# Attention with softmax maxima added by matrix products: the products on halves of the array, their transposes at later places, and a tail of zeros written by scatters

## The reference

```python
def _L0_xattn_ref(q, k, v, wq_w, wq_b, wk_w, wk_b, wv_w, wv_b, wo_w, wo_b):
    # H = 16 heads of DH = 8 channels
    wq = (q @ wq_w.T + wq_b).reshape(b, t, H, DH)
    wk = (k @ wk_w.T + wk_b).reshape(b, t, H, DH)
    wv = (v @ wv_w.T + wv_b).reshape(b, t, H, DH)
    scores = jnp.einsum('bthd,bshd->bhts', wq, wk) / jnp.sqrt(jnp.float32(DH))
    probs = jax.nn.softmax(scores, axis=-1)
    attn = jnp.einsum('bhts,bshd->bthd', probs, wv)
    return attn.reshape(b, t, d) @ wo_w.T + wo_b

def _L0_ffn_ref(x, Wg, W1, W2, W3):
    # E = 8 experts, TOP_K = 2
    logits = xf @ Wg
    top_w, top_i = jax.lax.top_k(logits, TOP_K)
    top_w = jax.nn.softmax(top_w, axis=-1)
    combine = jnp.einsum('nk,nke->ne', top_w, jax.nn.one_hot(top_i, E))
    h = jnp.einsum('nc,ech->enh', xf, W1)
    g = jnp.einsum('nc,ech->enh', xf, W2)
    y = jnp.einsum('enh,ehc->enc', jax.nn.silu(h) * g, W3)
    out = jnp.einsum('enc,ne->nc', y, combine)

x = x + jnp.tanh(g_xattn[0]) * _L0_xattn_ref(_layernorm(x), ctx, ctx, ...)
x = x + jnp.tanh(g_ffn[0]) * _L0_ffn_ref(_layernorm(x), ...)
```

## Time and profile before

| | |
|---|---|
| median of 3 runs | 519.75 us |
| lowest and highest | 516.56 and 519.78 us |
| the profiled execution | 516.52 us |
| its span | 514.4 us |
| PE, matmul busy | 465.3 us, 90% of the span |
| DVE busy | 388.0 us, 75% |
| ACT busy | 301.9 us, 59% |
| POOL busy | 222.6 us, 43% |
| mean granted clock | 0.993 |

### The profile page before, as it was taken

The page is one execution under the profiler, slowest core; times in us unless marked ns, Lnnn a source line. Parts: engine busy times, 40 slices in busy tenths (PEclk is TensorE's granted clock), DMA queues, the critical chain, the costliest instruction groups (busy, mean ns, idle before and its releaser), DMA issues. The chain is left out here.

```text
span 514.4 us, 14505 instructions
## 1 busy us (share of the span) xinstructions
PE 465.3 (90%) x4462; PEld 380.5 (74%) x4462; DVE 388.0 (75%) x1684; ACT 301.9 (59%) x755; POOL 222.6 (43%) x311
## 2 busy tenths in 40 slices
PE   2479999999999999899799999998998989899997
PEld 1257877777777787677687788767897877777996
DVE  4567788988889888767468658676799886677974
ACT  2377777777777775545365565466544547453553
POOL 2322155556565444545000177562668762224420
PEclk9999999999999999999899999999999999999999
DMA  8701001100001110135465344320000221000011
GB/s 245 299 11 53 13 32 41 38 31 36 36 31 37 34 52 24 43 114 164 135 180 168 97 134 124 91 78 24 22 27 16 57 57 48 11 2 1 1 42 42
DMA packets 45022, 34.60 MB, mean 67 GB/s; under 512 B 5922, under 2 KB 41122, under 8 KB 44708
## 3 DMA queue, kind: packets, MB, share of 16 engines
q1 hardware_dynamic: 30036, 20.55, 13.4%
q0 software_dynamic: 4128, 8.40, 5.3%
q10 hardware_dynamic: 10800, 4.92, 3.3%
HBM read 21.86 MB, written 11.99 MB: 66 GB/s over the span
## 5 line engine op out<-in xcount | busy, mean ns | idle before, releaser
L482 POOL DMA_INDIRECT sent<-xr,rowu x60 | 59.1, 986 | 67.6 <-DVE rowu L1041 53.6
L498 POOL DMA_INDIRECT yg<-done,gidx x64 | 64.3, 1004 | 31.5 <-issue 16.6
L1260 DVE TENSOR_TENSOR act<-sil,bank 128x256 f32<-128x256 f32 x71 | 29.8, 420 | 28.7 <-ACT sil L697 25.8
L931 DVE TENSOR_REDUCE mx<-bank 128x8 f32<-128x512 f32 x64 | 41.1, 683 | 11.0 <-PE bank L1694 11.0
L697 ACT ACTIVATE sil<-bank 128x256 f32<-128x256 f32 x71 | 27.3, 384 | 36.5 <-PE bank L1868 36.5
L464 POOL TENSOR_TENSOR ve<-mv,half 128x4 f32<-128x4 f32 (+1 forms) x40 | 8.9, 221 | 86.5 <-DVE mv L855 83.8
L1884 PE MATMUL bank<-f0w_s,aT 128*128 x284 | 45.1, 282 | 0.8 <-DVE yb L1266 0.8
L636 ACT ACTIVATE Pr<-bank 128x512 f32<-128x512 f32 x64 | 34.7, 597 | 13.5 <-PE bank L1708 13.5
L1884 PEld LDWEIGHTS bank<-f0w_s,aT 128*128 128x128 f32 x284 | 38.2, 195 | 1.7 <-issue 1.2
L1694 PE MATMUL bank<-QK 64*64 64x256 f32 x512 | 36.4, 401 | 2.9 <-ACT QK L626 2.9
L800 ACT ACTIVATE hg<-bank 128x512 f32<-128x512 f32 x32 | 19.1, 598 | 30.0 <-PE bank L2042 26.5
(11 more groups left out here) (253 smaller groups left out, 1309.6 us busy)
## 6 DMA issues: line engine op xcount, KB each, us to landing
xb<-sent SPq DMA_DIRECT2D x71, 64.0 KB
done<-yb ACTq DMA_DIRECT2D x71, 64.0 KB
cT<-ctx_t_dram SPq DMA_DIRECT2D x16, 128.0 KB
f0w_s<-f_w_dram SPq DMA_DIRECT2D x1, 2048.0 KB, 11.0
Pr<-ctx_t_dram SPq DMA_DIRECT2D x8, 256.0 KB
QK<-ctx_tok_dram SPq DMA_DIRECT2D x8, 256.0 KB
out_dram<-xs SPq DMA_DIRECT2D x8, 256.0 KB, 2.3
xs<-x_dram SPq DMA_DIRECT2D x2, 512.0 KB, 5.7
```

What stands on the lines that cost most here:

```text
L482: nc.gpsimd.indirect_dma_start(sent, bass.IndirectOffsetOnAxis(ap=rowu[:, s, 2 * k + c:2 * k + c + 1], axis=0), rows[:, c, :], None).then_ ...
L498: nc.gpsimd.indirect_dma_start(yg[:, s, j, :], None, done[0:NG1 * P, :] if u < UG else done, bass.IndirectOffsetOnAxis(ap=gidx[:, s, j:j + ...
L931: nc.vector.tensor_reduce(mx[:, g, :], bank[SC_BANK[g]][:].rearrange("p (m k) -> p m k", k=L), AX, ALU.max).then_inc(S("a_max"), 1)
```

## The change

What it does, by the pieces of the diff:

- `mxs` becomes 128 x 128 for each j, in a part of QK that nothing else uses in the attention. Its columns 0 to 7 and 8 to 15 hold the rounded maxima and their rests of g = 2j, columns 64 to 79 those of g = 2j + 1, and POOL writes zeros into the others once. The transpose (`a_mt`) takes all 128 columns, and ACT copies 128 partitions. So the maxima of g = 2j lie on partitions 0 to 63 and those of g = 2j + 1 on 64 to 127, and each product of `a_less` takes 64 rows as weights and 64 of the one `own_m` left.
- ACT no longer fills `mxT` with zeros and writes one version of `own_m`.
- `a_mt(u + 1, 0)` stands behind `r_lg(u - 2)` instead of ahead of it. `a_mt(u + 1, 1)` stood at the end of iteration u; now it stands in iteration u + 1 between the transposes of g = 0 and g = 1, and ACT's copy between the copies of g = 0 and g = 1.
- SP's `zero_after` is gone. `tail` has the row for each partition and expert, and POOL scatters 8 x 128 rows of zeros behind the last unit's sends, which no longer wait for blocks 13 to 16.

```diff
@@ constants
-    c[np.arange(32), C_MB + np.arange(32) % 16] = 1
+    c[p, C_MB + p % 8] = p % L < 16
@@ tiles
-        mxs = sb("mxs", [P, 2, 2, 16], F32R)
+        mxs = QK[:, U4 // 4, 0:2 * P].rearrange("p (j x) -> p j x", j=2)
...
-        tail = sb("tail", [1, E], U32)
+        tail = sb("tail", [P, E], U32)
@@ SP
-                sp.wait_ge(S("a_s"), 2 * UA)
+                sp.wait_ge(S("a_mt"), 2 * UA)
...
-            def zero_after(e):
-
-                if e == 0:
-                    sp.wait_ge(S("tail"), 1)
-                r = sp.value_load(tail[0:1, e:e + 1], min_val=e * REGION, max_val=e * REGION + TOKENS)
-                sp.dma_start(sent[bass.ds(r, P), :], zero[:]).then_inc(S("tails"), 16)
...
-                if 16 <= t < 16 + E // 2:
-                    zero_after(2 * (t - 16))
-                    zero_after(2 * (t - 16) + 1)
@@ POOL
+            nc.gpsimd.memset(mxs[:], 0.0).then_inc(fill, 1)
...
-            send(UA - 1, 1, (13, 14, 15, 16))
+            def zero_after(first, last):
+
+                for e in range(first, last):
+                    nc.gpsimd.indirect_dma_start(sent, bass.IndirectOffsetOnAxis(ap=tail[:, e:e + 1], axis=0), zero[:], None).then_inc(S("tails"), 16)
+
+            pool.wait_ge(zeroed, 16 * E)
+            send(UA - 1, 1)
+            wait_alone(pool, S("tail"), 1)
+            zero_after(0, E)
@@ ACT
-            for r in range(2):
-                nc.scalar.activation(own_m[:, r, :].rearrange("p (m k) -> p m k", k=L),
-                                     cst[:, C_MB + 8 * r:C_MB + 8 * r + 8].unsqueeze(2).to_broadcast([P, 8, L]), ACT.Copy)
-                nc.scalar.activation(mxT[:, r, :], ident, ACT.Copy, scale=0.0)
+            nc.scalar.activation(own_m[:, 0, :].rearrange("p (m k) -> p m k", k=L),
+                                 cst[:, C_MB:C_MB + 8].unsqueeze(2).to_broadcast([P, 8, L]), ACT.Copy)
...
-                nc.scalar.activation(mxT[0:32, j, :], bank[MT_BANK[j]][0:32, 0:P], ACT.Copy, scale=-1.0).then_inc(S("a_mts"), 1)
+                nc.scalar.activation(mxT[:, j, :], bank[MT_BANK[j]][:, 0:P], ACT.Copy, scale=-1.0).then_inc(S("a_mts"), 1)
...
                     a_pts(u, 0)
+                    a_mts(u, 1)
                     a_pts(u, 1)
...
-                if has(u + 1):
-                    a_mts(u + 1, 1)
@@ DVE
-                nc.vector.tensor_copy(mxs[:, j, 0, :], some).then_inc(S("a_ms"), 1)
+                nc.vector.tensor_copy(high.bitcast(F32R), some).then_inc(S("a_ms"), 1)
...
-                nc.vector.tensor_tensor(mxs[:, j, 1, :], some, mxs[:, j, 0, :], ALU.subtract).then_inc(S("a_ms"), 1)
+                nc.vector.tensor_tensor(low.bitcast(F32R), some, high, ALU.subtract).then_inc(S("a_ms"), 1)
...
-                    nc.vector.tensor_copy(tail[:], run[0:1, :]).then_inc(S("tail"), 1)
+                    nc.vector.tensor_scalar(tail[:], run[:], cst[:, C_P:C_P + 1], None, ALU.add).then_inc(S("tail"), 1)
@@ PE
-                nc.tensor.transpose(bank[MT_BANK[j]][0:32, 0:P], mxs[:, j].rearrange("p h m -> p (h m)").bitcast(F32), ident).then_inc(S("a_mt"), 1)
+                nc.tensor.transpose(bank[MT_BANK[j]][:, 0:P], mxs[:, j, :], ident).then_inc(S("a_mt"), 1)
...
-                    mm(bank[SC_BANK[2 * j + r]][:], mxT[:, j, :], own_m[:, r, :], start=False, stop=True,
+                    mm(bank[SC_BANK[2 * j + r]][:], mxT[L * r:L * (r + 1), j, :], own_m[L * r:L * (r + 1), 0, :], start=False, stop=True,
...
                     a_pt(u, s, 0)
+                    a_mt(u, 1)
                     a_pt(u, s, 1)
...
+                if has(u - 2):
+                    r_lg(u - 2)
                 if has(u + 1):
                     a_mt(u + 1, 0)
-                if has(u - 2):
-                    r_lg(u - 2)
...
-                if has(u + 1):
-                    a_mt(u + 1, 1)
```

More of the change, by code:

```diff
@@ L69 @@
 C_MB = C_QM + 2
-C_N = C_MB + 16
+C_N = C_MB + 8
 R_BO, R_BQV, R_BG = 0, 128, 256
@@ L407, in _ @@
                 if u == 1:
-                    sp.wait_ge(fill, 10)
+                    sp.wait_ge(fill, 11)
                     for e in range(E):
@@ L456, in _ @@
             nc.gpsimd.memset(w1c[:], 0.0).then_inc(fill, 1)
+            nc.gpsimd.memset(mxs[:], 0.0).then_inc(fill, 1)
             pool.dma_start(f0g_s[:], f0_wg).then_inc(ld_f0g, 16)
-            pool.wait_ge(fill, 10)
+            pool.wait_ge(fill, 11)
             def rstd(k, u, n):
@@ L648, in _ @@
             a.wait_ge(prep, 3)
-            a.wait_ge(fill, 10)
+            a.wait_ge(fill, 11)
             def r_xts(v):
@@ L897, in _ @@
             v.wait_ge(ld_attn, 64)
-            v.wait_ge(fill, 10)
+            v.wait_ge(fill, 11)
             nc.vector.tensor_copy(bvb[:], colv[:, BV:BV + 1].to_broadcast([P, P]))
@@ L933, in a_split @@
             def a_split(u, j):
-                some = mx[:, 2 * j:2 * j + 2, :].rearrange("p g m -> p (g m)")
+                some = mx[:, 2 * j:2 * j + 2, :]
+                high, low = (mxs[:, j, :].rearrange("p (r x) -> p r x", r=2)[:, :, 8 * k:8 * k + 8] for k in range(2))
                 v.wait_ge(S("a_max"), u * 4 + (2 * j + 2))
-                nc.vector.tensor_copy(mxs[:, j, 0, :], some).then_inc(S("a_ms"), 1)
+                nc.vector.tensor_copy(high.bitcast(F32R), some).then_inc(S("a_ms"), 1)
                 v.wait_ge(S("a_ms"), u * 4 + (2 * j + 1))
-                nc.vector.tensor_tensor(mxs[:, j, 1, :], some, mxs[:, j, 0, :], ALU.subtract).then_inc(S("a_ms"), 1)
+                nc.vector.tensor_tensor(low.bitcast(F32R), some, high, ALU.subtract).then_inc(S("a_ms"), 1)
             def a_rec(u):
```

## The result

| | before | changed |
|---|---|---|
| median | 518.86 us of 6 runs (516.56 to 519.97) | 507.29 us of 6 runs (504.81 to 507.94) |
| ratio | | 0.977, interval 0.974 to 0.980 |
| profiled execution, span | 516.52, 514.4 us | 504.81, 502.9 us |
| start of the expert stage's block 0 | 210.33 us | 204.71 us |
| block 18 to block 21 | 9.39 us | 5.26 us |

The change makes the kernel 11.6 us faster by the medians. The starts of PE's first transpose of a block split the 11.5 us that the profiled execution's span lost: 5.6 in the attention, 4.1 between blocks 18 and 21, and 1.8 that no part of the change accounts for, 0.75 between blocks 0 and 18 (35.85 us before, 35.10 now) and 1.0 behind block 21 (258.83 and 257.83). In the first of these stretches the granted clock of before stood at 0.50 for 3.4 us (from 217.4); the changed kernel's profiled execution has no such fall.

What follows compares the result with a forecast made beforehand. PE's queue, busy 90% of the span, was taken as the bound. Terms 3.8 + 3.4 + 1.1 + 4.4 = 12.7 us gave 503.8 from the profiled execution or 507.0 from the median; forecast 505.5 us, range 502 to 510.

Steps and rivals of the forecast that it cites:

- The halves, 3.8 us: Attention: 512-column product pairs on array halves save 0.22 and 0.02 us, 16 units x 0.24 = 3.8 us on PE's path.
- The later places, 3.4 + 1.1: Attention: moving the maxima's transposes later cuts PE's waits, 3.4 us over four loop pairs and 1.1 us outside the loop.
- none at the turn: At the loop's turn, PE would have no wait left before the transposed maxima; elsewhere at most 0.4 us.
- DVE just keeps up: Attention loop: of DVE's slack, some 1.4 us a pair, the gains use 1.3, so DVE would not hold PE back.
- The rival on DVE's pace: Attention loop: DVE sets the pace, its eight units gain nothing, 5.3 us are lost, time 511; chance 0.12.
- The zeros, 4.4: Expert stage, blocks 18 to 21: zeros moved from SP to POOL save 4.9 us, less 0.5 stall at block 25: 4.4.
- The clock's share included: Expert stage: the 4.9 us gain at blocks 18 to 21 includes time from a halved clock lasting some 2 us.
- Halves in sequence: Rival, attention: the two half-array products run one after the other, costing 7 us, time 512.5; chance 0.12.
- the slow case: Rival, attention: half arrays handle the reduced float type at the float rate, 17 us lost, time 527; chance 0.06.
- Cheaper changes of form: Rival, attention: changes of tiling form cost less and the turn gives all it has, 3.7 us more, 502; chance 0.05.
- Late zeros: Rival, expert stage: zeros come too late, a 3 us stall at block 25 and a clock fall cancel 4.4; 510; chance 0.05.
- The starting point: Whole kernel: gains taken from the profiled 516.5 us give 503.8, from the 519.75 median 507.0; 505.5 chosen between.

Runs made afterwards that it cites:

- last sends behind blocks: The changed kernel with the last unit's two sends waiting for blocks 13 to 16 again, as before the change; 507.69 us, ratio 0.977.
- POOL's step moved: The changed kernel with POOL's 128 x 512 subtraction for the gate's weights (w12_low) moved from behind the sends to between two small steps, units 1 to 8; 504.9 us.
- fastest kernel: The changed kernel with POOL's w12_low subtraction moved beside the maxima and four DVE bookkeeping steps moved behind the first split of the maxima; 502.41 us, ratio 0.966.

## Why the prediction was right, and where it was not

The time (507.3 for 505.5) came out within the range. The terms did so less evenly, and in part it was luck: the attention gave 5.6 us (5.9 from unit 0 to unit 15) for 8.3, and 1.8 us of the profiled gain of 11.5 came where no term had counted anything.

*The halves, 3.8 us: the step that failed.* "16 units x 0.24", "on PE's path", is right in its size, 0.28 measured in the late units, 0.25 of it in the first pair and 0.03 in the second, and wrong in the path: it holds only where PE has no wait behind it. Alone the halves gave 0.1% by the ratio, 0.4 us, and that can't be told from nothing. On top of the places they bring block 0 from 206.22 to 204.71, 1.5 us, and unit 0 to unit 15 from 166.50 to 164.79, 1.7 us: 0.4 of this in the loop's eight units and 1.3 in the others.

*The later places, 3.4 + 1.1.* From unit 0's product with the values to unit 15's it is 170.67 us before and 166.23 with the places alone: 4.4 us, for 4.5. Inside, the sum was off both ways. The loop's units gave 4.0: a pair fell by 1.04 us (23.98 to 22.94) and not by 0.84. The edges gave 0.5 for 1.1. At the start the covered wait fell by 0.58 us (1.84 to 1.26), but the next one grew by 0.40 (0.97 to 1.37). Behind the loop, units 11 to 15 take 41.05 us before and with the places: the wait of 0.73 only made room for one for DVE's table, which stands ahead of the ranks (0.58 with the places alone; the line is the changed kernel's),

```profile
166.34 0.18 PE L1762 MATMUL bank<-chosen,upb 128*128 128x8 bf16 x1 [0.53 <-DVE table L1142]
```

and the first transpose's later place cost 0.36 in the iteration of unit 14 (193.49 above, 0.37 there). No queries and keys are left to be made in it, and the logits, which stood between the transpose and the pair of products, now stand ahead of both, so the pair waits for ACT's copy. The prediction had no term for this. Of the waits that were to be left, the one of 0.4 is 0.22 (at 114.55); "none at the turn" missed by 0.19.

*"DVE just keeps up".* It is where the prediction should have stopped. DVE's slack was counted once for both gains and taken to be free for either. It belonged to the ring, and the places used it up; there was none for the halves. The rival on DVE's pace named this, but with a price of 5.3 us ("the loop's eight units gain nothing"). From unit 3 to unit 11 they gained 4.2 of these 5.3 (95.22 to 91.03). Loop pairs of 22.7 were said, 22.90 came.

*The zeros, 4.4.* 4.1 us between blocks 18 and 21 (9.39 to 5.26), and as much in the kernel with the zeros alone. Two terms were off and nearly cancelled. Three blocks take 5.26 and not 4.5, so less was there to win. And no stall came at block 25. The margin hardly changed: from the last zeros' issue to PE's block 25 it is 6.8 us (244.2 to 251.0), where the prediction had 6.1. What differs is the load, taken to need 3.4 us, which was there within 2.04 of its issue in the kernel with the last sends behind blocks. "The clock's share included" was not needed, and the fall lasted 3.4 us and not some 2: the kernels with the halves or the places alone take 9.2 us there at a granted clock of 1.00. The gap is SP's lost lead; the low clock of the earlier trace rows took the place of a part of the waiting.

*The rivals.* Halves in sequence and the slow case fell: both products of the reduced type stream at once, at the rate of the whole array. (The slow case's own sum gives 526, not 527.) Cheaper changes of form fell with the 0.03 us of the second pair. Late zeros need 3 us more.

*The starting point.* Between 503.8 and 507.0 the prediction took the middle. The changed kernel's profiled execution is its fastest (504.81, clock 1.00), and the others, at 0.99 to 0.997, lie 0.9 to 3.1 us above; the median stands at 507.3. The 12.7 of the sum against the median of all runs of before, 518.86, would have given 506.2.

## What to carry to other kernels

When two engines wait for each other in turn, their waits are one ring and not two stores of slack: ask for every saving whether it lies on the stretch from one engine's wait to what it hands over, for else it only lengthens the next wait. A gain that shows in the written-out units and not in the loop is the sign of it; it comes back in full once the ring is shorter than the engine's own work, as the halves did here (0.27 us a unit in the loop). To get there, take out of the chain between the two engines what no one nearby needs, and look for operations that take much longer in the loop than outside, as the subtraction of 0.16 us did that took up to 1.32.

## What was not expected of the hardware

- A VectorE subtraction of 128 x 2 with both inputs in SBUF took 0.88 to 1.32 us beside a GpSimd subtraction of 128 x 512 with two inputs and ended with it, and 0.16 us otherwise; VectorE's reductions from PSUM kept their 1.28 us beside the same GpSimd instruction. The Trainium skill, "SBUF — State Buffer", Who interferes with whom, says just this of a VectorE instruction with two SBUF inputs; the trace agrees, with up to 1.16 us of blocking for each. It does not do so for every pair: beside GpSimd's power of 128 x 2 with two inputs (L458, 0.73 us in the loop) VectorE's operations with two SBUF inputs of L987 took 0.16 to 0.19 us, 23 times from 60 to 205 us in the changed kernel. Why these two cases differ no run here shows.
- The granted clock falls to 0.50 (1.2 GHz) for some microseconds at places that differ from execution to execution: twice for 3.4 us in the profiled execution of before (from 217.4 and from 251.5 us), never in that of the changed kernel. In the fastest kernel's, around unit 0:

```profile
34.00:37.86 3.86, 3.40 (x23) 1.71 (x24) 0.35 (x2) 2.44 (x6) 0.00 (x0) 0.78 0.00 0
37.86:51.75 13.89, 13.89 (x152) 11.06 (x148) 8.72 (x34) 7.46 (x17) 3.52 (x9) 0.69 0.17 49
```

  The unit takes 11.6 us at full clock, so 2.3 us are lost (the clock stands at 0.50 from 36.1 to 46.4), and block 0 of that kernel in the table would stand at 199.6 or before. These three falls follow a stretch in which PE had waited (here 1.58 us before the maxima), but the kernels with the halves or the places alone have the same gap at block 19 and no fall behind it. That kernel's executions at a mean clock of 0.997 took 501.26 and 501.52 us, this one at 0.98 took 505.47: such falls go with most of the spread of a few us. In twelve of the fourteen profiled executions a fall of 3.4 or 3.5 us begins within 7 us behind the start of block 0; the changed kernel's first and the one with POOL's step moved have none there. Only the fastest kernel's has one ahead of block 0, so that the table's other times of block 0 are free of them. What sets them off no run here shows.
